# The first pair of a graph layer as eight plain block products, with the matrix made in column halves

## The reference

```
h   = relu(layernorm(x, over N))                      # 64 x 128 x 1024
avg = mean of h over the 64 samples                   # a vector of 128 for each of the 1024 nodes,
                                                      # each divided by its norm
sim = (avg.T @ avg + 1) / 2
A   = (sim + gumbel0 > 1 - sim + gumbel1)             # 1024 x 1024, zeros and ones
nmask  = clip(A + A.T + I, 0, 1);  common = nmask @ nmask.T
W   = A * (common^2 / max(common)) where an edge is valid, else 0
deg = W.sum(axis=0);  Wn = deg^-1/2 * W * deg^-1/2
out = x + Wn.T applied over the nodes of (h @ weight) + bias      # for each of 64 samples
```

## Time and profile before

| what | value |
|---|---|
| median of 3 runs | 878.57 us (878.41 to 878.64) |
| the profiled execution | 877.09 us, span 875.1 us |
| mean granted PE clock | 0.978 |
| PE busy | 820.3 us, 94% of the span |
| DVE / ACT / POOL busy | 581.0 / 509.9 / 321.7 us |
| chain that ended last | PE 78%, DVE 8%, issue 6%, POOL 5%, ACT 2% |

### The profile page before, as it was taken

One profiled execution on the slowest core, in us unless ns is written; L12 is line 12 of the kernel. 1 busy time (PEld: TensorE's weight loads), 2 busy tenths in 40 slices (PEclk: granted clock), 3 DMA queues, 4 the chain that ended last, 5 costly groups with the idle time before them and its releaser, 6 DMA issues.

```text
span 875.1 us, 13556 instructions
## 1 busy us (share of the span) xinstructions
PE 820.3 (94%) x4740; PEld 427.7 (49%) x4740; DVE 581.0 (66%) x667; ACT 509.9 (58%) x523; POOL 321.7 (37%) x260
## 2 busy tenths in 40 slices
PE   4999899943899999999999999999999999999997
PEld 3544455531454555455545555554555455545553
DVE  7999766869855655666566656555665666566653
ACT  3888804847565665666555645565665666456531
POOL 4788710232033333333343333333333433343320
PEclk9999999976899999999999999999999999999999
DMA  8999802000633222222222223333222222222111
GB/s 348 409 408 396 362 1 73 1 1 0 236 122 113 107 97 97 97 97 96 96 96 96 96 104 135 109 110 111 102 96 96 96 96 96 96 96 97 51 69 74
DMA packets 29545, 111.04 MB, mean 127 GB/s; under 512 B 3408, under 2 KB 3536, under 8 KB 28496
## 3 DMA queue, kind: packets, MB, share of 16 engines
q1 hardware_dynamic: 29520, 110.70, 34.2%
HBM read 77.14 MB, written 33.55 MB: 126 GB/s over the span
## 4 chain that ended last, share of the span: by engine, by line
PE 78%; DVE 8%; issue 6%; POOL 5%; ACT 2%; DMA 0%; POOLq 0%; ACTq 0%; DVEq 0%; SPq 0%
PE ps L789 66%; PE ps L742 8%; DVE stats L864 4%; POOL rstd L335 1%; POOL zbuf L345 1%; PE ps L671 1%; DVE xring L1054 1%; DVE xring L1016 1%; ACT xring L563 0%; ACT zbuf L407 0%; ACT a L568 0%; PE ps L646 0%; PE ps L685 0%; POOL zbuf L374 0%; DVE moments L870 0%
## 5 line engine op out<-in xcount | busy, mean ns | idle before, releaser
L789 PE MATMUL ps<-a,ybuf 128*128 128x512 f16 x2688 | 592.4, 380 | 22.4 <-DVE a L1022 14.8
L789 PEld LDWEIGHTS ps<-a,ybuf 128*128 128x128 f16 x2688 | 261.5, 98 | 329.4 <-issue 19.2
L947 DVE TENSOR_TENSOR ybuf<-zbuf,ybuf 128x1024 f16<-128x1024 f32 (+1 forms) x128 | 168.0, 1312 | 165.9 <-ACT ybuf L480 165.9
L371 POOL TENSOR_TENSOR zbuf<-zbuf 128x512 f32<-128x512 f32 x32 | 40.9, 1277 | 418.1 <-ACT zbuf L466 418.1
L480 ACT ACTIVATE ybuf<-zbuf 128x1024 f16<-128x1024 f32 (+1 forms) x128 | 121.6, 950 | 115.5 <-POOL zbuf L376 102.5
L494 ACT ACTIVATE obuf<-ps,bias_sb,w_out 128x512 f32<-128x512 f32 x64 | 49.4, 772 | 121.6 <-PE ps L789 121.6
L936 DVE TENSOR_TENSOR hring<-hring 128x1024 f16<-128x1024 f32 x56 | 68.6, 1224 | 58.7 <-ACT hring L452 58.7
L742 PEld LDWEIGHTS ps<-w,hring 128*128 128x128 f16 x1344 | 79.7, 98 | 13.4 <-issue 0.4
L742 PE MATMUL ps<-w,hring 128*128 128x128 f16 x1344 | 84.2, 219 | 0.3 <-DVE k L979 0.3
L1083 DVE TENSOR_TENSOR obuf<-obuf,xring 128x1024 f32<-128x1024 f32 x64 | 78.4, 1225 | 2.8
L374 POOL TENSOR_TENSOR zbuf<-zbuf 128x512 f32<-128x512 f32 x32 | 71.7, 2240 | 0.0
(11 more groups left out here) (125 smaller groups left out, 629.3 us busy)
## 6 DMA issues: line engine op xcount, KB each, us to landing
xring<-in_x_dram SPq DMA_DIRECT2D x96, 512.0 KB, 4.5
out_dram<-obuf SPq DMA_DIRECT2D x64, 512.0 KB, 2.9
ybuf<-in_x_dram SPq DMA_DIRECT2D x28, 512.0 KB, 9.8
a<-in_L_gnn_gumbel_dram SPq DMA_DIRECT2D x7, 1024.0 KB, 14.4
obuf<-in_x_dram SPq DMA_DIRECT2D x7, 512.0 KB, 5.9
obuf<-in_L_gnn_gumbel_dram SPq DMA_DIRECT2D x1, 1024.0 KB, 22.6
w<-in_adj_dram SPq DMA_DIRECT2D x1, 64.0 KB, 1.8
bias_sb<-in_L_gnn_bias_dram SPq DMA_DIRECT2D x1, 0.5 KB, 2.1
```

Source lines behind the costliest of these rows:

```text
L789: mm = nc.tensor.matmul(bank[q % 2], y16[:, q % 2, yk, u, c * P:(c + 1) * P], a16[:, ak, mat, c, :], start=(start and c == yk == ak == 0), ...
L947: nc.vector.tensor_tensor(y16[:, q % 2, 1, a:a + n, :], z[:, a + 1:a + 1 + n, :], y16[:, q % 2, 0, a:a + n, :], ALU.subtract).then_inc(s_y, 1)
```

## The change

Pair 0 is no longer made by the scheme of seven. `first_pair` does its two samples as eight plain block products with the matrix's own blocks, in the order A11 (slot 0), A12 (held for a while in slot 6), A21 (slot 1), A22 (slot 2), both samples after each other: 96 matmuls. Pair 0 so needs no sums on POOL, no combined matrix and no `partial`; four ACT instructions (`FIRST_OUT`) write its outputs. The combined matrices (slots 3, 4, 5, 6) are made behind the four plain ones, and pair 1 waits for them. The upper row tiles are scaled and squared in column halves of 512, the left halves first. L391's subtraction moves from POOL to DVE. The feature products, `z_of` and `relu2` of pair 2, and `relu2` of pair 3, move ahead of or among the making of the matrix; for that, samples 4 to 7 get early loads into `obuf`. `xw_of(0, 1, 1)` moves from the seventh to the fifth row tile of `common`. 14 matmuls of zeros (`stay_awake`) are put ahead of `turn(1)`.

```
-            y_high(0, 0, 3)
+            z_of(0, 1, 0)
+            y_high(0, 1, 0)
             turned(5)
             degree_of(4)
-            z_of(0, 1, 0)
-            y_high(0, 1, 0)
+            z_of(0, 1, 1)
+            y_high(0, 1, 1)
...
-            y_high(0, 1, 2)
             y_high(0, 1, 3)
+            relu2(0, 2, 0)
+            relu2(0, 2, 1)
...
             for c in range(HC):
-                square(rows_hi, 0, c)
+                square(c, rows_hi[:, c, LO])
             act.wait_ge(s_a32, HC)
             high(0, rows_hi[:, :, LO])
-            square(rows_lo, 1, 0)
-            square(rows_lo, 1, 1)
+            z_of(0, 2, 0)
+            for c in range(HC):
+                square(HC + c, rows_hi[:, c, HI])
+            act.wait_ge(s_a32, C)
+            act.wait_ge(s_e, C + HC)
+            high(A12, rows_hi[:, :, HI])
+            for c in range(HC):
+                square(C + c, rows_lo[:, c, :])
+            z_of(0, 2, 1)
+            act.wait_ge(s_a32, C + HC)
+            high(1, rows_lo[:, :, LO])
+            high(2, rows_lo[:, :, HI])
             act.wait_ge(s_t, 1)
             high(3, spare)
...
             act.wait_ge(s_t, 2)
             high(4, rows_hi[:, :, LO])
-            act.wait_ge(s_t3, 1)
+            act.wait_ge(s_t, 3)
             high(5, rows_hi[:, :, HI])
-            high(1, rows_lo[:, :, LO])
+            relu2(0, 3, 0)
+            act.wait_ge(s_t, 4)
+            act.wait_ge(s_mm, 14 + 3)
+            high(6, spare)
             act.wait_ge(s_wout, 1)
-            partial(0, 0, 0)
-            partial(0, 0, 1)
-            partial(0, 0, 2)
-            act.wait_ge(s_t, 3)
-            high(6, spare)
-            relu2(0, 2, 0)
-            relu2(0, 2, 1)
-            for q in range(1, PAIRS):
+            act.wait_ge(s_hhi, 6)
+            for n, (b, m, bank) in enumerate(FIRST_OUT):
+                act.wait_ge(s_mm, 14 + 4 + n)
+                nc.scalar.activation(o[0][b][:, m], bank, ACT.Identity, bias=bias_sb[:, 0:1],
+                                     scale=w_out[:, 0:1]).then_inc(s_first, 1)
+            relu2(0, 3, 1)
+            act.wait_ge(s_hhi, 7)
+            act_pair(0, 1, True, False, False)
+            for q in range(2, PAIRS):
...
-                if e == 6:
+                if e == 4:
                     xw_of(0, 1, 1)
             pe.wait_ge(s_m, C)
+            stay_awake(ps[:, 3, 0:P], 14)
             turn(1)
+            spread(1)
...
-            spread(1)
+            xw_of(0, 2, 0)
+            xw_of(0, 2, 1)
...
+            def first_pair():
+
+                pe.wait_ge(s_y, 8)
+                for k, mat in enumerate(FIRST):
+                    pe.wait_ge(s_alo, k + 1)
+                    for b in (0, 1):
+                        u = ((0, 3), (1, 2))[k // 2][b]
+                        bank = FIRST_OUT[2 * (k % 2) + b][2]
+                        for c in range(HC):
+                            for yk, ak in ((0, 0), (0, 1), (1, 0)):
+                                mm = nc.tensor.matmul(bank, y16[:, 0, yk, u, c * P:(c + 1) * P],
+                                                      a16[:, ak, mat, c, :], start=(k < 2 and c == yk == ak == 0),
+                                                      stop=(k >= 2 and c == HC - 1 and yk == 1), skip_group_check=True)
+                        if k + b > 0:
+                            mm.then_inc(s_mm, 1)
...
             top_of(1)
-            y_low(0, 1, 2)
-            dve.wait_ge(s_qrow, 2)
-            rooted(rows_hi, 0, 0)
+            y_low(0, 1, 3)
             dve.wait_ge(s_topb, 2)
...
+            h_low(0, 2, 0)
+            for half, m in enumerate((LO, HI)):
+                dve.wait_ge(s_qrow, half + 1)
+                for c in range(HC):
+                    rooted(rows_hi, 0, c, m)
+            h_low(0, 2, 1)
+            low(0, 0, rows_hi[:, :, LO])
+            for c in range(HC):
+                rooted(rows_lo, 1, c)
+            low(1, A12, rows_hi[:, :, HI])
+            dve.wait_ge(s_a32, C)
             nc.vector.tensor_tensor(spare, rows_hi[:, :, HI], rows_hi[:, :, LO], ALU.subtract).then_inc(s_t, 1)
...
+            low(2, 1, rows_lo[:, :, LO])
+            low(3, 2, rows_lo[:, :, HI])
             dve.wait_ge(s_t, 1)
-            dve.wait_ge(s_alo, 1)
+            dve.wait_ge(s_alo, 2)
             nc.vector.tensor_tensor(rows_hi[:, :, LO], rows_lo[:, :, HI], spare, ALU.subtract).then_inc(s_t, 1)
-            low(2, rows_lo[:, :, HI])
-            low(4, rows_hi[:, :, LO])
+            nc.vector.tensor_tensor(rows_hi[:, :, HI], rows_lo[:, :, HI], rows_hi[:, :, HI],
+                                    ALU.subtract).then_inc(s_t, 1)
+            low(4, 3, spare)
             dve.wait_ge(s_t, 2)
-            dve.wait_ge(s_alo, 2)
+            dve.wait_ge(s_alo, 5)
             nc.vector.tensor_tensor(spare, rows_lo[:, :, LO], rows_hi[:, :, LO], ALU.subtract).then_inc(s_t, 1)
-            low(5, rows_hi[:, :, HI])
-            low(1, rows_lo[:, :, LO])
+            low(5, 4, rows_hi[:, :, LO])
+            low(6, 5, rows_hi[:, :, HI])
+            h_low(0, 3, 0)
+            low(7, 6, spare)
...
             add_x(0, 0, 0)
-            h_low(0, 2, 1)
-            lower1(0, 0)
             add_x(0, 0, 1)
-            for q in range(1, PAIRS):
+            h_low(0, 3, 1)
+            dve_pair(0, 1, True, False)
+            for q in range(2, PAIRS):
```

More of the change, by code:

```diff
@@ L144, in gnn_kernel @@
         spare = hring[:, 3:5, :].rearrange("p a (b n) -> p (a b) n", b=2)
-        x_first = {j: obuf[:, j, :] for j in (1, 2, 3)}
+        x_first = {j: obuf[:, j % 4, :] for j in range(1, BODY)}
         z = zbuf[:, :, :].rearrange("p a (b n) -> p (a b) n", b=2)
@@ L170, in gnn_kernel @@
         ps_xw2 = pair[3]
+        FIRST_OUT = ((0, LO, ps_a[0]), (1, LO, ps_b[0]), (0, HI, ps_d[0]), (1, HI, ps_a[1]))
         s_consts = sem("consts_loaded")
@@ L228, in gnn_kernel @@
         s_t = sem("t_ready")
-        s_t3 = sem("t3_ready")
         s_ahi = sem("a_high_ready")
         s_alo = sem("a_low_ready")
-        s_xf = [sem(f"x_first_loaded{j}") for j in (1, 2, 3)]
+        s_xf = {j: sem(f"x_first_loaded{j}") for j in range(1, BODY)}
+        s_first = sem("first_pair_block_read")
         s_h32 = sem("h32_ready")
@@ L282, in _ @@
             sp.wait_ge(s_adj, C)
[L283 to L286, removed]
+            for j in range(1, BODY):
+                if j > 4:
+                    sp.wait_ge(s_hhi, j - 4)
+                sp.dma_start(x_first[j], x[j]).then_inc(s_xf[j], 16)
+            sp.wait_ge(s_t, 4)
+            for j in (0, 1, 2, 3):
+                sp.dma_start(xring[:, j, :], x[j]).then_inc(s_x2[j], 16)
+            sp.wait_ge(s_alo, 7)
             for j in (4, 5, 6, 7):
-                sp.dma_start(xring[:, j, :], x[j]).then_inc(s_x2[j], 16)
-            sp.wait_ge(s_alo, 6)
-            for j in (0, 1, 2, 3):
                 sp.dma_start(xring[:, j, :], x[j]).then_inc(s_x2[j], 16)
@@ L506, in act_pair @@
                 if ahead1:
-                    z_of(i, q + 1, 1)
+                    if evict:
+                        z_of(i, q + 1, 1)
                     y_high(i, q + 1, 1)
@@ L554, in _, with square @@
             degree_of(7)
-            y_high(0, 1, 2)
             y_high(0, 1, 3)
-            def square(rows, k, c):
-                if k == 0 and c == 0:
+            relu2(0, 2, 0)
+            relu2(0, 2, 1)
+            def square(n, part):
+                if n == 0:
                     act.wait_ge(s_kap, 3)
-                act.wait_ge(s_e, HC * k + c + 1)
-                nc.scalar.activation(rows[:, c, :], rows[:, c, :], ACT.Square,
-                                     scale=kappa[:, 0:1]).then_inc(s_a32, 1)
+                act.wait_ge(s_e, n + 1)
+                nc.scalar.activation(part, part, ACT.Square, scale=kappa[:, 0:1]).then_inc(s_a32, 1)
             def high(mat, src):
@@ L820, in pe_pair @@
                 product(q, 5, 5, ps_b, False)
-                made(1)
+                if second:
+                    pe.wait_ge(s_first, 4)
                 product(q, 1, 1, ps_a, True)
@@ L984, in _ @@
             mask(1)
-            y_low(0, 0, 0)
+            y_low_first(0)
             mask_t(1)
@@ L989, in _ @@
             mask_t(2)
-            y_low(0, 0, 1)
+            y_low_first(1)
             mask(3)
@@ L1005, in _ @@
             mask(7)
+            y_low(0, 1, 2)
             root(0, 0, 6)
-            y_low(0, 1, 1)
             bound(1, 6, C)
@@ L1115, in dve_pair @@
                 add_x(i, q, 1)
-            upper0(0, 0)
-            low(6, spare)
-            upper1(0, 0)
-            y_low(0, 1, 3)
-            h_low(0, 2, 0)
-            lower0(0, 0)
             add_x(0, 0, 0)
-            h_low(0, 2, 1)
-            lower1(0, 0)
             add_x(0, 0, 1)
-            for q in range(1, PAIRS):
+            h_low(0, 3, 1)
+            dve_pair(0, 1, True, False)
+            for q in range(2, PAIRS):
```

89 lines of the change are left out of this document (42 added, 47 removed).

## The result

Over 20 runs of each, taken in turns, the changed kernel has a median of 875.4 us against 877.33 us before. The medians are 1.9 us apart. The ratio is 0.9975, with a 95% interval of 0.9965 to 0.9985: faster by 0.25%, which is 2.2 us, or 1.3 to 3.1. The forecast was 1.6 us, a ratio of 0.9982. The profiled execution of the changed kernel took 873.94 us; its span is 872.2 us.

What follows compares the result with a forecast made beforehand. Bound: PE from pair 2 on, so only pair 2's start counts. Last stall's end 241.3 + 12.95 + 1.6 = 255.9 instead of 257.5 us; 878.57 - 1.6 = 877.0 us, range 873.2 to 880.8.

Steps and rivals of the forecast that it cites:

- this case: The prediction's main case: pair 2 starts at 255.9 instead of 257.5 us, 1.6 us gained; chance 0.45.
- PE's new wait for `z_of(0, 1, 0)`: After the fifth tile of common, PE waits for z_of on ACT: a new stall of 1.7 us.
- The largest root: End of the row tiles: its maximum on DVE comes at 189.0 us against 188.3 before.
- The fillers at full clock: Ahead of turn(1) on PE: 14 matmuls as 28 instructions at 0.116 us each, 3.2 us.
- A11's residue: The matrix's first residue, low(0) on DVE, ends at 202.1 us, 207.4 before.
- The first block product: PE's start on A11 in pair 0: near 203.5 us.
- POOL's turns: POOL's sums of pair 2 come between DVE's residues and subtractions; three waits cost DVE 3.3 us together.
- `partial(0, 1, 0)`: On ACT behind relu2(0,3,1), which needs DVE's h_low(0,3,0): it ends at 241.1 us and is what PE waits for last.
- The stall of PE: In pair 1, before its third product: PE stands from 234.7 to 241.3 us, 6.6 us.
- The restart: After the pair 1 stall, PE's 60 matmuls cost 1.6 us beyond 12.95 by starting at half clock.
- The half-clock fillers: Rival: fillers ahead of turn(1) take 6.2 us, all behind is 3.1 later, 880.4 us; chance 0.20.
- The change gives nothing: Rival kept inside the main case: A11 is 5 us earlier, and the order behind it gives most back; no own chance.

Runs made afterwards that it cites:

- e6: The changed kernel with relu2(0,2,1) on ACT behind the first high and z_of(0,2,0), and h_low(0,2,1) on DVE behind the lower rooted; 872.89 us, 0.9944 of the kernel before.
- e8: The changed kernel with the two products of A11 made twice, 24 matmuls more, same result; 874.93 us, 0.997 of the kernel before.
- e3: The changed kernel with POOL's z_sums(2) held back until the eighth low; 871.93 us, 0.9933 of the kernel before.
- e2: The changed kernel with partial(0,1,0), y_high(0,2,0) and partial(0,1,1) ahead of relu2(0,3,1) on ACT; 869.26 us, 0.99 of the kernel before.
- e5: The changed kernel with xw_of(0,1,1) after the sixth tile of common, not the fifth; 875.32 us, 0.9974 of the kernel before.
- e7: The changed kernel with the edits of e2, e3, e5 and e6 together; 867.96 us, 0.9894 of the kernel before.
- e11: The kernel of e10 with the 14 filler matmuls kept; 868.48 us, 0.9898 of the kernel before.
- e4: The kernel before with only POOL's subtraction (L391) given to DVE, right behind L1054; 873.35 us, 0.9949 of the kernel before.
- e1: The changed kernel without the 14 filler matmuls; 874.94 us, 0.9966 of the kernel before.
- e9: The changed kernel with xw_of(0,1,1) after the sixth tile of common and without the fillers; 872.84 us, 0.9943 of the kernel before.
- e10: The kernel of e7 without the fillers and with xw_of(0,2,1) on PE between the products of A11 and A12; 865.8 us, 0.986 of the kernel before.
- e12: The kernel of e10 with y_low(0,2,0), h_low(0,3,1), upper0(0,1), upper1(0,1) ahead of both add_x of pair 0 on DVE; 862.72 us, 0.9834 of the kernel before.

## Why the prediction was right

**Right in its place.** The change moved pair 2's start, and only that: 1.4 us in the profiles, 1.6 forecast. The time itself, 875.4 us, is 1.6 below the 877.0 forecast and just under the bounds given to this case (875.8 to 878.2). Most of that is the starting point: 878.57 was a median of three runs, and over 20 runs the kernel before has 877.33.

The steps that carried the forecast, each against its own number, times with the 1.5 us added:

- PE's new wait for `z_of(0, 1, 0)`: 1.53 us, 1.7 forecast.
- The largest root: at 188.1, 189.0 forecast and 188.3 before. This step was mis-sized. `bound(0, 0, 6)` ran without being blocked, as POOL's last sum had ended at 182.5, 0.5 us ahead of it, and the last hand-over from POOL took 0.1 us, not the 0.5 of before.
- The fillers at full clock: 3.39 us, 3.2 forecast. The first `relu2` ahead of the squares; half-squares at 0.61 each (2.54 for four): as forecast.
- A11's residue ends at 201.5, 202.1 forecast, 207.4 before; A12's at 210.6, 211.1 forecast.
- The first block product: at 202.7, 203.5 forecast. The forecast had overlooked a wait: PE stood 6.33 us for ACT's `z_of(0, 2, 0)`, ran the feature product at the lower clock (2.72 us for 1.50) and so came to A11 1.2 us behind its residue. e6 and e8 show that this cost nothing.
- POOL's turns: 3.0 us, 3.3 forecast; shown to be the cause by e3.
- `partial(0, 1, 0)` begins at 239.7, where the forecast had 240.3, and it stands behind `relu2(0, 3, 1)` and `h_low(0, 3, 0)`, shown by e2.
- The stall of PE: 4.75 us, 6.6 forecast. PE fell to the lower clock right behind the 2.3 us wait ahead of A21 too, and its 48 matmuls took 12.22 us for 10.4, so it came later to the stall. It changed nothing, since the end of the stall is ACT's.
- The restart: 60 matmuls in 15.6 us, 2.7 above full clock. I took 1.6, the mean of two restarts of before. This is the other mis-sized term. The stall ended 0.8 us earlier than forecast, above all by the earlier root, and the restart cost 1.1 more. That the two cancelled, so that 1.6 and 1.4 lie so close, is luck.

The Trainium skill (SBUF — State Buffer, the section "Who interferes with whom") says that a VectorE operation with two SBUF inputs and a GpSimd one that reads SBUF exclude each other. The trace agrees: POOL's sums cost DVE 3.0 us, where the mean of L947 would have given 0.5, and the two engines took turns.

**The rivals.** The half-clock fillers did not come in the profiled run of the change, but they came in e5, e7 and e11, at 5.0 us instead of 6.2. So this rival is real. Which case a kernel meets isn't settled by the length of the idle time; in these traces it goes with the place of `xw_of(0, 1, 1)`. Behind the fifth tile of `common` the fillers took 3.39 us in all five kernels (the change, e2, e3, e6, e8), behind the sixth 5.02 in all three. Why is not shown. "The change gives nothing" was nearly right about the part in the title: e6 and e8 show that neither the early first product nor 24 matmuls more on PE count, and e4 that moving L391 alone gives more than the whole. The gain of 1.4 us is what was left over when three waits of the new order had been paid, which taken out singly are worth 2.5 (e6), 4.0 (e3) and 6.2 us (e2); part of each is the clock behind the last stall.

**Left open.** The change was not run with L391 left on POOL, nor the eight products or the column halves by themselves, so it isn't shown that either of them brings anything. The paths come from one execution of each kernel; whether all 20 runs of the change meet the fast fillers was not seen.

## What to carry to other kernels

Before a start-up is rearranged to bring the first matmul forward, follow each later instruction that PE will need and ask what stands in front of it on its own engine: here a preparation for pair 3, put ahead of a 0.8 us read for pair 1, cost four times what the change gained. Where DVE and POOL both have operations with two SBUF inputs, count each of POOL's as if it stood in DVE's list (here 1.0 us for each of three sums), and put it where DVE is idle. An early part that waits for data is not on the path merely because it is first: double it, or delay it, and see whether the end moves.

## What the runs showed of the hardware that was not expected

- The same 28 filler pieces behind the same idle time of PE (2.51 and 2.45 us) took 3.39 us in five programs and 5.02 in three others.
- PE's lower clock came right after a wait of only 2.3 us (0.53 in the window 217 to 218 of the change; the 48 matmuls behind that wait take 12.1 to 12.2 us also in e1, e2, e5 and e9), and not after one of 1.5 us (10.53 in e3, e10, e11 and e12). The restart behind 4.75 us of idle cost 2.7 us, more than those behind 14.8 and 7.6 us before (1.9 and 1.3).
- Where the clock level falls is not the same in each run: four matmuls at 109 us took 3.65 or 1.99 us, 1.5 us of the whole time. Over 20 runs the change's times span 873.35 to 877.91 us, more than the effect that was to be measured. So the whole time of a single profile can't give it; the time from the mark could.
